# First phase of a four-stage image kernel: weight loads behind the first norm steps, their preparation inside the main loop, and 49-row matmuls issued in pairs from two halves of a tile

## The reference

```python
x = x + L0_conv(_ln_c(x), ...)     # _ln_c: over the 48 channels, eps 1e-6
# inside L0_conv:
z = einsum('bchw,dc->bdhw', x, in_w) + in_b          # 48 -> 96 channels
z = depthwise_conv3x3(z, dw_w, 'SAME') + dw_b
z = z * sigmoid(z)
x_dbl = einsum('bkdl,ked->bkel', four orders of z, x_proj_weight)
```

## Time and profile before

| what | us |
|---|---|
| median of 3 runs | 1723.23 |
| lowest and highest run | 1716.86, 1728.10 |
| profiled execution, its own time | 1725.15 |
| span of the profiled execution | 1723.4 |
| first norm product on PE starts | 11.06 |
| first unit on PE starts | 44.59 |
| first instruction of `scan0_phase` on ACT | 226.89 |

### The profile page before, as it was taken

One profiled execution on the slowest core, in us unless ns is written; L12 is line 12 of the kernel. 1 busy time (PEld: TensorE's weight loads), 2 busy tenths in 40 slices (PEclk: granted clock), 3 DMA queues, 4 the chain that ended last, 5 costly groups with the idle time before them and its releaser, 6 DMA issues. The chain is left out here.

```text
span 1723.4 us, 15970 instructions
## 1 busy us (share of the span) xinstructions
PE 1308.8 (76%) x3822; PEld 439.7 (26%) x3822; DVE 1295.8 (75%) x1358; ACT 1169.0 (68%) x1791; POOL 964.0 (56%) x507
## 2 busy tenths in 40 slices
PE   3999928566484378764789988888888888774996
PEld 2343301101010155541222222222222222111563
DVE  1455539879698267750399999999999999993675
ACT  2566338668586167764888888888888888740554
POOL 4100016958869433212788888998888888960000
PEclk9999955555555599987688798888888888655897
DMA  5343240020200323311777777777777777633562
GB/s 144 97 127 109 71 134 24 2 98 0 100 0 0 104 66 95 95 52 54 185 173 168 180 165 169 167 171 173 177 174 172 177 176 165 152 79 85 122 169 72
DMA packets 137305, 200.02 MB, mean 116 GB/s; under 512 B 27387, under 2 KB 69629, under 8 KB 136450
## 3 DMA queue, kind: packets, MB, share of 16 engines
q1 hardware_dynamic: 135380, 196.53, 46.0%
q10 hardware_dynamic: 1854, 2.70, 0.6%
HBM read 145.55 MB, written 53.63 MB: 116 GB/s over the span
## 5 line engine op out<-in xcount | busy, mean ns | idle before, releaser
L1775 DVE TENSOR_TENSOR_SCAN m_h<-m_qa,m_state,m_ub 128x512 f32<-128x512 f32 x384 | 463.9, 1262 | 14.5 <-POOL m_ub L1387 10.3
L1387 POOL TENSOR_TENSOR m_ub<-m_dlb,m_bt 128x1536 f32<-128x1536 f32 x128 | 438.4, 3444 | 15.2 <-DVE m_h L1775 11.4
L1736 ACT ACTIVATE m_qa<-m_dlb,k_a 128x512 f32<-128x512 f32 x384 | 253.9, 682 | 87.6 <-DVE m_h L1775 86.3
L1132 POOL TENSOR_TENSOR b_u<-b_dl,b_z 128x1024 f32<-128x1024 f32 x48 | 125.8, 2623 | 245.1 <-DMA b_z<-scratch_z 198.5
L1589 PE MATMUL m_qc<-m_bcr,k_selc 32*128 32x512 f32 x256 | 163.0, 720 | 101.1 <-DVE m_g L1786 101.0
L1786 DVE TENSOR_TENSOR m_g<-m_h,m_qc 128x1536 f32<-128x1536 f32 x128 | 221.6, 1732 | 11.6 <-issue 5.9
L1606 PE MATMUL m_qy<-m_g,k_seld 128*32 128x512 f32 x768 | 175.6, 769 | 0.0
L969 PE MATMUL b_qb<-b_bc,k_pack_sel 96*128 96x512 bf16 x96 | 78.6, 819 | 108.0 <-DVE b_u L1053 108.0
L1027 ACT ACTIVATE b_qa<-b_dl,b_a 128x512 f32<-128x512 f32 x96 | 65.5, 684 | 91.3 <-DVE b_h L1068 78.5
L1532 PE MATMUL m_qf<-m_cva,k_conv 113*96 113x504 f32 (+1 forms) x192 | 106.5, 699 | 19.9 <-DMA m_cvb<-scratch_xpad 19.9
L1068 DVE TENSOR_TENSOR_SCAN b_h<-b_qa,b_h,b_u 128x512 f32<-128x512 f32 x84 | 107.1, 1276 | 0.1
(11 more groups left out here) (185 smaller groups left out, 2637.3 us busy)
## 6 DMA issues: line engine op xcount, KB each, us to landing
m_dlb<-scratch_dldu SPq DMA_DIRECT2D x128, 384.0 KB, 10.2
m_bt<-scratch_brow SPq DMA_DIRECT2D x128, 256.0 KB, 5.9
scratch_dldu<-m_dldu SPq DMA_DIRECT2D x32, 384.0 KB, 3.2
scratch_z<-a_z SPq DMA_DIRECT2D x24, 256.0 KB, 5.9
b_z<-scratch_z SPq DMA_DIRECT2D x3, 2048.0 KB, 8.8
scratch_y<-b_yrow SPq DMA_DIRECT2D x12, 512.0 KB, 2.9
c_y<-scratch_y SPq DMA_DIRECT2D x16, 384.0 KB, 3.4
scratch_gate<-m_gt SPq DMA_DIRECT2D x32, 192.0 KB, 3.6
```

The lines of the kernel that those rows point to most:

```text
L1132: nc.gpsimd.tensor_tensor(by_column(u[s][:], col), by_column(dl[s][:], col), seen(z[:], col, piece), ALU.mult).then_inc(u_ready, 1)
L1387: nc.gpsimd.tensor_tensor(ub[k % 3][:], dlb[u % 2][:, J:2 * J, :], bcast(bt[u % 2][:, n, :], J), ALU.mult).then_inc(ub_ready, 1)
L1736: nc.scalar.activation(q_a[:, j, :], dlb[u % 2][:, j, :], ACT.Exp, scale=G["a1"][:, j, n:n + 1]).then_inc(da, 1)
L1775: nc.vector.tensor_tensor_scan(h[k % 3][:, j, :], q_a[:, j, :], ub[k % 3][:, j, :], state[:, k % NS, j:j + 1], ALU.mult, ALU.add).then_inc ...
```

## The change

It has four parts. (1) ACT issues only the two early loads first, and the ten others behind the first five norm steps, ahead of the units. The load of `inner0` goes: the inner product reads its weights from `pack_cin`. (2) PE issues the inner products of two units, b and b+1, together at every even unit: the first from partitions 0 to 48, the second from partitions 64 to 112 (whose copy in `pack_cin` is a second set of the same weights). That needs the image row 8i+9 in the lower half, so the second load of rows has 576 in place of 512 columns (441 in place of 392 KB). (3) PE's seven weight products move behind unit 25, DVE's 22 operations behind unit 26, ACT's five behind the last norm step (unit 21), where the table that they need is loaded. (4) Their results lie in the first PSUM tile.

```diff
     def act_load(self, act):
         for dst, src in self.early:
             act.dma_start(dst, src).then_inc(self.early_loaded, 16)
+
+    def act_load_rest(self, act):
         for dst, src in self.loads:
             act.dma_start(dst, src).then_inc(self.loaded, 16)
...
-        self.early += [(G["inner0"][:], D["pack_cin"][0:C + 1, place("pack_cin", "c0_in")])]
...
+    def inner_of(self, pe, s, b, u):
+        rows, at = (slice(0, C + 1), 2 * W) if b % 2 == 0 else (slice(64, CIN), W)
+        pe.wait_ge(self.low_out, freed(u))
+        self.nc.tensor.matmul(self.q1[b % 2][:], self.inner[rows, :], self.cv[s][rows, b, at:at + CH],
+                              start=True, stop=True).then_inc(self.inner_mm, 1)
+
     def products(self, pe, s, b, u):
         r = b % 2
-
-        pe.wait_ge(self.low_out, freed(u))
-        self.nc.tensor.matmul(self.q1[r][:], self.inner[:], self.cv[s][0:C + 1, b, 2 * W:2 * W + CH],
-                              start=True, stop=True).then_inc(self.inner_mm, 1)
+        if r == 0:
+            self.inner_of(pe, s, b, u)
+            self.inner_of(pe, s, b + 1, u + 1)
+
         pe.wait_ge(self.tapped, freed(u))
...
-    sp.dma_start(cv[64:64 + C + 1, :, 0:CH],
-                 xpad[:, :, bass.ds(i * ROWS + 1, ROWS), :].rearrange("b c r w -> c b (r w)")).then_inc(sem, 16)
+    sp.dma_start(cv[64:64 + C + 1, :, 0:CH + W],
+                 xpad[:, :, bass.ds(i * ROWS + 1, ROWS + 1), :].rearrange("b c r w -> c b (r w)")).then_inc(sem, 16)
...
+PREPARE = 25
...
-        weights = Weights(nc, m, D, G, qn[0][:, 0, 0:1], qn[1][0:DI, 0, 0:DI], qn[2])
+        weights = Weights(nc, m, D, G, qn[0][:, 0, 0:1], qn[0][0:DI, 0, P:P + DI], qn[0][:, 1:4, :])
...
                 if norm_at(u - 1) is not None:
                     var(norm_at(u - 1))
-            pe.wait_ge(left, done(NCH - 1))
-            pe.wait_ge(ready, NCS)
-            weights.pe_bias(pe)
+                if u == PREPARE:
+                    pe.wait_ge(ready, NCS)
+                    weights.pe_bias(pe)
...
                     norm.act_rstd(act, n - 1, slot(n - 1))
+            weights.act_load_rest(act)
             act.preload_act_table_set(SILU_SET)
...
                     norm.act_rstd(act, norm_at(u - 1), 0)
+                    if norm_at(u - 1) == NCS - 1:
+                        weights.act_alog(act)
                     act.preload_act_table_set(SILU_SET)
-            act.preload_act_table_set(LOG_EXP_SET)
-            weights.act_alog(act)
...
                 if u >= 4 and (u - 4) % B == B - 1:
                     split_lo((u - 4) // B)
-            weights.dve_make(dve)
+                if u == PREPARE + 1:
+                    weights.dve_make(dve)
```

More of the change, by code:

```diff
@@ L598, in front0_phase @@
         loaded, stored = ([m.sem(f"a_{n}{s}") for s in range(2)] for n in ("loaded", "stored"))
-        conv = Conv(nc, m, "a", G["conv0"], G["inner0"], G["c0_low"], cv, [bank(1, r) for r in range(2)],
+        conv = Conv(nc, m, "a", G["conv0"], G["c0_in"], G["c0_low"], cv, [bank(1, r) for r in range(2)],
                     [bank(2, r) for r in range(2)])
-        weights = Weights(nc, m, D, G, qn[0][:, 0, 0:1], qn[1][0:DI, 0, 0:DI], qn[2])
+        weights = Weights(nc, m, D, G, qn[0][:, 0, 0:1], qn[0][0:DI, 0, P:P + DI], qn[0][:, 1:4, :])
         nst = 16 * (J + 2)
@@ L1959, in views @@
     return found
-KEPT = [("conv0", [CIN, 3, DI], F32), ("conv1", [CIN, 3, DI], F32), ("inner0", [C + 1, DI], F32),
+KEPT = [("conv0", [CIN, 3, DI], F32), ("conv1", [CIN, 3, DI], F32),
         ("low1", [CIN, DI], F32), ("left1", [C + 1, DI], F32), ("wdt", [DI + 1, P], F32), ("gate64", [64 + C, DI], F32), ("dmat", [DI, DI], F32),
```

## The result

The changed kernel takes 1700.35 us (median of 4 runs, 1692.39 to 1704.64) where the kernel before took 1721.39 beside it. The ratio is 0.9863, 95% interval [0.9838, 0.9888]. A second series of both gave 1700.31 against 1722.85, ratio 0.9861 [0.9835, 0.9887]. So the gain by the ratio is 1.37% of 1723.23, 23.6 us (19.3 to 27.9 by the interval; the two medians of the first series lie 21.0 us apart), where I had forecast 17.9. The time lies inside the stated range, and 1705.3 is 5 us too high.

The account below looks back on a forecast made before the run. It took a load-and-norm chain to bound the front and PE alone the units; 2.0 (front) + 17.8 (pairs) - 2.3 - 0.3 (preparation) + 0.7 (tail) = 17.9 us off 1723.23 gave about 1705.3 us, range 1698 to 1713.

Parts of the forecast that it names:

- Pairs: Unit loop on PE: the second inner product of a pair is free, 1.11 us saved each, 17.8 us for sixteen.
- Front: Start of `front0_phase`, up to the first unit: moving weight loads back lets ACT square earlier, 2.0 us gained.
- Of the competition I know only the bounds ... so I take 3.7: First row loads: weight loads beside them cost 3.7 us, half of the upper bound of 7.5 us.
- issued at 30.4: Front: the first row loads go out at 30.4 us instead of 35.69, with 1.3 us allowed for a straggling DMA engine.
- my bound of 6.6 us for the whole gain: Front: PE waits 6.59 us for the squares, so at most 6.6 us are to be had.
- wrong if the first unit starts at 39: Sign against the forecast: the first unit, expected at 42 to 44 us, starting at 39 or at 47 us.
- Preparation: Weight preparation moved into the unit loop: 2.3 us lost on PE, 0.3 us on taps, 0.7 us gained at the tail.
- the tail: End of `front0_phase`: DVE's end at 223.03 us goes, SP's stores stay at 222.3, 0.7 us gained.
- No overlap: Rival, unit loop: a wait stands between a pair's products, pairs give 4.0 us, time 1719.1 us; chance 0.08.
- The row loads never became the limit: Rival, unit loop: row loads at 17 us, twice the time seen, make PE wait, time 1729 us; chance 0.04.
- The weights don't delay the row loads: Rival, front: DMA engines have room, the first unit comes the whole 6.6 us earlier, time 1700.7 us; chance 0.18.

Follow-up runs that it names:

- after: The changed kernel with all four parts, against the kernel before: ratio 0.9863 [0.9838, 0.9888], 1700.35 us; units 0 to 3 took 26.22 us.
- after_again: The changed kernel run and profiled once more, unchanged, against the kernel before: ratio 0.9861 [0.9835, 0.9887], 1700.31 us; units 0 to 3 took 21.40 us.
- pairs_only: The kernel before plus only the paired inner products, weight loads and preparation left where they were: ratio 0.9859 [0.9815, 0.9904] to the kernel before.
- cin_split: The changed kernel with the load of `pack_cin` cut into 112 rows and 1 row: ratio 0.9883 [0.9842, 0.9924] to the kernel before.
- best2: The changed kernel with `dtw` loaded and split early, `pack_cin` loaded as 112 and 1 rows, bias products before the last projection, DVE's conversions behind the loop: 1696.42 us.
- split_early: The changed kernel with `dtw` as ACT's first load, so POOL splits it before the first taps: ratio 0.9869 [0.9832, 0.9907] to the kernel before.
- pool_held: The changed kernel with POOL's splits and shapes held until the taps of unit 8 are done: ratio 0.9863 [0.9828, 0.9898] to the kernel before.
- best3: The changed kernel with early `dtw` split, `pack_cin` cut, bias products before the last projection, conversions behind the loop, late weights on SP behind two groups' row loads: 1689.37 us.
- undo_prepare: The changed kernel with the weight preparation moved back behind the unit loop: ratio 0.9880 [0.9844, 0.9916] to the kernel before.
- same_half: The changed kernel with both inner products of a pair reading partitions 0 to 48: ratio 0.9953 [0.9934, 0.9973] to the kernel before.
- loads_only: The kernel before plus only the ten weight loads moved behind the first five norm steps, no pairs: ratio 0.9972 [0.9950, 0.9994] to the kernel before.

## Why the prediction was right in part

- **Pairs: right, slightly small.** Forecast 1.11 us each, measured 1.19; 16 make 19.0 and not 17.8. PE remains the limit. I had worked the 1.11 out from single rows; two neighbouring units of the trace with the entry costs on both sides would have been the better measure.
- **Front: the number right by luck, two of its steps wrong.** With 2.4 us of pairs taken off, unit 4 starts 1.6 us earlier in after (63.37 against 67.41) and 6.5 us earlier in after_again; the forecast was 2.0. The first failed step is "Of the competition I know only the bounds ... so I take 3.7". With "issued at 30.4" it put the first unit at 43.3 and it came at 37.15. The rows went out 3 us sooner than I said, past my bound of 6.6 us for the whole gain, and the weights 1.4 us sooner, so they stood 4.3 us behind the rows and not 2.6. The row loads took 9.76 us against 9.46 in pairs_only, where no weights compete. In the eight profiles with the weights some 4 us behind they took 9.9 us in the mean (8.8 to 10.5), and in the three with none beside them 9.2, with 0.3 added for the smaller load of the kernel before: some 0.6 us, not 3.7. The competition has the size that I gave it with the weights 2.8 us behind (cin_split, best2), but not in this placement. By my own test ("wrong if the first unit starts at 39") this step fell.
- **The second failed step is one that isn't there.** I followed the weight loads on ACT's queue and on the DMA engines, but not to who waits for them. POOL's split waits for the last one, moves from 31.82 to 44.78 us, and holds DVE up. In the prediction the time of units 0 to 3 changes by the pairs alone. Units 0 to 3 take 19.9 to 21.0 us without it (pairs_only, split_early, pool_held, best2, best3), 21.4 in after_again and 26.2 in after: up to 6 us, of which part is the granted clock that falls behind a longer wait. In after this took back most of what the missing competition had given. So two errors cancelled, and the number looked right by luck.
- **Preparation: sign right, size too large.** 1.66 + 0.38 - 0.69 = 1.35 us by the rows (the last term is the tail, 12.52 to 11.83 us from the last projection to the mark, forecast 0.7), 1.0 by undo_prepare, forecast 1.9.
- **Rivals.** "No overlap" fell with same_half. The row loads never became the limit: PE is busy for the whole of 64 to 100 us. "The weights don't delay the row loads" gave 1700.7, next to the measured time; its mechanism holds nearly for this placement (the first unit came 7.44 us earlier, it said 6.6), but it too missed POOL, so its number is luck as well.
- **The 5 us missed** consist of 1.2 from the pairs, 0.6 from the preparation, up to 4.5 from the front in executions where the stretch is cheap, and the open 3 us behind the mark. How the last two share, and what the clock did in each run, is not settled.

## What to carry to other kernels

When a load is moved, list every engine that waits for its semaphore and what that engine will then run beside; the cost may come from a third engine whose instruction meets a shared port, it may differ from run to run, and a wait that lets TensorE's clock fall costs more than its own length. Large transfers that are not urgent are best issued behind the urgent ones: here 1.46 MB of weights 11 us or 4 us behind the row loads left these at 8.8 to 10.5 us, and 2.8 us behind them made them 12.8 to 13.7. Products of half height from both halves of the partitions are worth pairing wherever PE limits.

## What was unexpected in the hardware

- Two DVE instructions of 96x504 with both tensors in SBUF took 4.07 to 5.50 us beside POOL's 13x1536 subtraction and casts, and 1.51 us alone; two of 113x288 took 3.71 us and 0.82. POOL lost little: its subtraction took at most 3.49 us beside the taps against 3.09 without them, its cast at most 1.99 against 1.45. DVE instructions with one operand in PSUM kept their 0.73 us.
- A transfer of 113 partitions kept about one of sixteen DMA engines busy (share 0.07, 26 GB/s from 15 to 18 us); split into 112 and 1 it was over before that stage (0.00).
- A wait of PE of 2.40 us (in loads_only 1.81) was followed by a granted clock of 0.50, waits of 1.19 and 1.52 us were not. The clock also fell to 0.50 from 180 to 185 us in same_half while PE was busy throughout. At 0.50 the three 113-row products took up to 5.38 us in place of 2.79.
